# Chunk sums in two halves around the second edge layer, slot messages in two buffers, window additions ahead of the comparison

## The reference

```python
h = jnp.maximum(_layernorm(x), 0.0)
for l in range(5):                                    # on x = h
    h = _leaky(x @ W1[l] + b1[l]) @ W2[l] + b2[l]
    e = _leaky(edge_attr @ We1[l] + be1[l]) @ We2[l] + be2[l]
    msg = h[src] * e * dot_scale[l]
    agg = jax.ops.segment_sum(msg, dst, num_segments=n)
    out = x + agg * res_w[l]
    x = layernorm(out) * ln_g[l] + ln_b[l]
# the result is the input x plus the last x
```

## Time and profile before

| | us |
|---|---|
| median of 3 runs | 6610.09 |
| lowest and highest | 6605.63, 6611.65 |
| the profiled execution | 6615.82 |
| its span | 6614.0 |
| PE, DVE, ACT, POOL busy | 5622.6, 5148.4, 1133.9, 4527.2 |

### The profile page before, as it was taken

One profiled execution on the slowest core, in us unless ns is written; L12 is line 12 of the kernel. 1 busy time (PEld: TensorE's weight loads), 2 busy tenths in 40 slices (PEclk: granted clock), 3 DMA queues, 4 the chain that ended last, 5 costly groups with the idle time before them and its releaser, 6 DMA issues.

```text
span 6614.0 us, 169076 instructions
## 1 busy us (share of the span) xinstructions
PE 5622.6 (85%) x63332; PEld 3676.7 (56%) x63333; DVE 5148.4 (78%) x7991; ACT 1133.9 (17%) x1726; POOL 4527.2 (68%) x4793
## 2 busy tenths in 40 slices
PE   6776899988888788888878888888898887888887
PEld 2223444456666555666655666655566665556665
DVE  8997544688887688888768888867888875888886
ACT  0000211111122211112211112221111222111111
POOL 5777777666677377777727777746777773777775
PEclk9997555799999799999979999988999997999998
DMA  3112399755566355656635655644565563666664
GB/s 135 26 26 47 78 240 242 185 131 138 138 148 152 96 132 136 142 141 154 159 80 133 145 143 143 162 112 116 129 147 142 148 161 78 139 147 156 151 171 110
DMA packets 733545, 886.20 MB, mean 134 GB/s; under 512 B 325488, under 2 KB 502976, under 8 KB 731568
## 3 DMA queue, kind: packets, MB, share of 16 engines
q1 hardware_dynamic: 568480, 703.64, 40.8%
q0 software_dynamic: 152144, 154.93, 12.4%
q10 hardware_dynamic: 12096, 16.53, 0.8%
HBM read 749.51 MB, written 125.06 MB: 132 GB/s over the span
## 4 chain that ended last, share of the span: by engine, by line
PE 54%; DVE 21%; issue 15%; DVEq 4%; ACT 3%; DMA 1%; POOL 0%; ACTq 0%; SPq 0%; POOLq 0%
PE bank L980 14%; PE bank L976 8%; PE bank L1029 7%; PE bank L1053 5%; PE bank L922 4%; PE bank L879 3%; DVE arena L1662 3%; PE bank L1016 3%; PE bank L860 2%; PE bank L845 2%; DVEq L1782 2%; DVE arena L1750 2%; ACT arena L1241 2%; DVE arena L1670 2%; DVE arena L1408 2%
## 5 line engine op out<-in xcount | busy, mean ns | idle before, releaser
L793 POOL DMA_INDIRECT arena<-h_rows,src x3855 | 3674.3, 953 | 1693.5 <-issue 1250.7
L980 PEld LDWEIGHTS bank<-w2s,arena 128*128 128x128 f32 x8960 | 1175.7, 210 | 772.3 <-DVE arena L1750 437.2
L980 PE MATMUL bank<-w2s,arena 128*128 128x128 f32 x8960 | 1307.0, 303 | 208.2 <-DVE arena L1750 191.4
L780 POOL DMA_INDIRECT slots<-arena,slot_index x792 | 787.2, 994 | 267.2 <-issue 241.3
L976 PE MATMUL bank<-nodes_state,edge_w 64*128 64x512 f32 x980 | 598.4, 693 | 307.3 <-DVE nodes_state L1718 142.6
L1053 PEld LDWEIGHTS bank<-arena 112*64 112x64 f32 x20160 | 640.4, 138 | 267.0 <-issue 245.1
L1053 PE MATMUL bank<-arena 112*64 112x64 f32 x20160 | 725.8, 225 | 60.1 <-issue 54.2
L976 PE MATMUL bank<-x_packed,edge_w 64*128 64x512 f32 x1260 | 740.1, 669 | 16.4 <-ACT std L1190 15.6
L1241 ACT ACTIVATE arena<-bank,tenth 128x512 f32<-128x512 f32 x490 | 335.5, 685 | 2296.6 <-PE bank L976 2296.6
L1662 DVE SCALAR_TENSOR_TENSOR arena<-bank,edge_w,arena 128x512 f32<-128x512 f32 x490 | 366.7, 748 | 424.1 <-ACT arena L1241 421.4
L1670 DVE TENSOR_TENSOR x_packed<-bank,slot_rel 128x2880 f32<-128x2880 f32 (+8 forms) x315 | 588.9, 1870 | 15.8 <-issue 15.8
(11 more groups left out here) (198 smaller groups left out, 5615.6 us busy)
## 6 DMA issues: line engine op xcount, KB each, us to landing
arena<-slot_pick SPq DMA_DIRECT2D x630, 448.0 KB
arena<-h_rows SPq DMA_DIRECT2D x630, 224.0 KB
x_packed<-slot_attr SPq DMA_DIRECT2D x630, 128.0 KB
nodes_state<-attr_t SPq DMA_DIRECT2D x485, 128.0 KB
arena<-h_rows,src POOLq DMA_INDIRECT x3855
slot_pick<-arena SPq DMA_DIRECT2D x126, 448.0 KB
x_packed<-slots SPq DMA_DIRECT2D x127, 136.0 KB, 4.9
slots<-arena SPq DMA_DIRECT2D x9, 1904.0 KB, 22.1
```

The source lines that it names most:

```text
L780: pool.indirect_dma_start(slots, bass.IndirectOffsetOnAxis(ap=slot_index[:, t:t + 1], axis=0), records[:, v, j, :], None).then_inc(record_ ...
L793: pool.indirect_dma_start(to[0:n, at:at + D], None, table, bass.IndirectOffsetOnAxis(ap=index[0:n, t:t + 1], axis=0)).then_inc(landed(t), 16)
L980: mm = pe.matmul(to[:, j * P:(j + 1) * P], acts[:, j * TILE:(j + 1) * TILE], w2s[:, :], start=True, stop=True)
```

## The change

The slot message gets a second buffer (`slot_msg`), in a part of SBUF that is free in the layers, and its writer no longer waits for sums. `chunk_sums` takes a range of its four parts: the first half of a step's sums stays where all of them were, the second half goes into the next step, behind the hidden layers and ahead of the second edge layer. At a chunk's end both halves are in the chunk's last step, the second behind the gathers. On VectorE the window additions, with the reading of the window's start, move ahead of "middle" and of the one-hot of places; that one-hot now waits for the chunk sums of the step before the last, whose places it overwrites.

```diff
--- before.py
+++ after.py
@@ -168,7 +168,7 @@
 
         x_packed = sb("x_packed", [P, NHALF])
         late, at = {}, 0
-        for name, n in dict(place=TPG * WMAX, tenth=HALF, attr=2 * HALF, x=TN, spill_pick=WMAX, spill_msg=HALF).items():
+        for name, n in dict(place=TPG * WMAX, tenth=HALF, attr=2 * HALF, x=TN, spill_pick=WMAX, spill_msg=HALF, msg=HALF).items():
             late[name] = x_packed[:, at:at + n]
             at += n
         assert at <= NHALF
@@ -257,6 +257,7 @@
         hid_tenth = [area("hid_tenth"), late["tenth"]]
         slot_e = area("slot_e")
         msg = area("msg").rearrange("p (k c) -> p k c", k=2)
+        slot_msg = [msg[:, 1, :], late["msg"]]
 
 
         WIDE = 4 * BUCKETS
@@ -1018,21 +1019,21 @@
                             if j == TPH - 1:
                                 mm.then_inc(win_ready, 1)
 
-                def chunk_sums(i):
+                def chunk_sums(i, begin, end):
                     c = i // BG
                     w = widths[c]
-                    for j in range(TPH):
+                    for j in range(begin, end):
                         for side in range(2):
                             at, k = (2 * j + side) * D, 2 * j + side
                             for half in range(2):
                                 slots_of = slice(half * D, (half + 1) * D)
-                                mm = pe.matmul(sum_ps[half][side * D:(side + 1) * D, 0:w], msg[slots_of, 1, at:at + D],
+                                mm = pe.matmul(sum_ps[half][side * D:(side + 1) * D, 0:w], slot_msg[i % 2][slots_of, at:at + D],
                                                slot_places[i % 2][slots_of, k * w:(k + 1) * w],
                                                start=(i % BG == 0 and j == 0),
                                                stop=(ends_chunk(i) and j == TPH - 1 and side == 1))
                                 if j == TPH - 1:
                                     mm.then_inc(sum_ready, 1)
-                    if ends_chunk(i):
+                    if ends_chunk(i) and end == TPH:
                         pe.wait_ge(spill_picked, l * CHUNKS + c + 1)
                         pe.wait_ge(spill_msg_ready, l + 1)
                         own_wait(pe, "pe")
@@ -1071,6 +1072,8 @@
                     if k is not None:
                         pe.wait_ge(slot_attr_landed[k % 2], 16 * (l * (NB // 2) + k // 2 + 1))
                         hidden_of(1, k, NB, slot_attr_in[:, k % 2, :])
+                    if b_at(s - 1) is not None and not ends_chunk(s - 1):
+                        chunk_sums(s - 1, TPH // 2, TPH)
                     now, m = a_at(s), a_at(s + 1)
                     if now == SPILL_AT:
                         pe.wait_ge(spill_msg_ready, l + 1)
@@ -1092,11 +1095,13 @@
                     if b_at(s) is not None:
                         if k is None:
                             own_wait(pe, "pe")
-                        chunk_sums(s)
+                        chunk_sums(s, 0, TPH // 2)
                     part("middle")
                     if k is not None:
                         pe.wait_ge(slot_e_biased, l * NB + k + 1)
                         gathered(k)
+                    if b_at(s) is not None and ends_chunk(s):
+                        chunk_sums(s, TPH // 2, TPH)
 
                 k = l + 1
 
@@ -1752,9 +1757,7 @@
                     if i is not None:
                         dve.wait_ge(slot_e_biased, l * NB + i + 1)
                         dve.wait_ge(source_ready, 2 * (l * NB + i + 1))
-                        if i > 0:
-                            dve.wait_ge(sum_ready, 4 * (l * (NB + CHUNKS) + i + i // BG))
-                        dve.tensor_tensor(msg[:, 1, :], slot_e, slot_ps[:, :], ALU.mult).then_inc(slot_msg_ready, 1)
+                        dve.tensor_tensor(slot_msg[i % 2], slot_e, slot_ps[:, :], ALU.mult).then_inc(slot_msg_ready, 1)
                     m, i = a_at(s + 1), b_at(s + 1)
                     if m is not None and m != SPILL_AT:
                         at = real(m) * TPG
@@ -1768,20 +1771,22 @@
                     if m is not None:
                         dve.wait_ge(e_ready, l * GA + m + 1)
                         edge_biased(e_ps[:, :], e_ps[:, :]).then_inc(e_biased, 1)
+                    if k is not None and k != SPILL_AT:
+                        group = GB0 + real(k)
+                        window_start[:] = [dve.value_load(start_i[0:1, 2 * group + side:2 * group + side + 1],
+                                                          min_val=0, max_val=NPAD) for side in range(2)]
+                        window_added(s, k)
                     part("middle")
                     if i is not None:
                         w = widths[i // BG]
+                        if i > 1:
+                            dve.wait_ge(sum_ready, 4 * (l * (NB + CHUNKS) + i - 1 + (i - 1) // BG))
                         one_hot(slot_places[i % 2][:, 0:TPG * w].rearrange("p (t w) -> p t w", w=w), TPG, w,
                                 slot_rel[:, i * TPG:(i + 1) * TPG])
                         if ends_chunk(i):
                             c = i // BG
                             t = 2 * c * SPILL_CAP // TILE
                             one_hot(spill_pick[:, 0:w].unsqueeze(1), 1, w, spill_rel[:, t:t + 1]).then_inc(spill_picked, 1)
-                    if k is not None and k != SPILL_AT:
-                        group = GB0 + real(k)
-                        window_start[:] = [dve.value_load(start_i[0:1, 2 * group + side:2 * group + side + 1],
-                                                          min_val=0, max_val=NPAD) for side in range(2)]
-                        window_added(s, k)
                     if ends_chunk(s):
                         chunk_added(s)
```

## The result

| | us |
|---|---|
| before: median (lowest to highest) | 6611.65 (6605.63 to 6620.89) |
| after: median of 5 runs (lowest to highest) | 6644.18 (6640.62 to 6656.99) |
| ratio of after to before, 95% interval | 1.0052 (1.0037 to 1.0067) |
| the profiled execution, its span | 6640.62, 6638.7 |

The change makes the kernel 0.5% slower. The prediction said 55 us faster; the time is inside its range and on the wrong side.

A forecast was written before the change was run, and what follows sets the result against it. TensorE and VectorE hand work to each other, neither full; a step is as long as the later one. Seams 0, plain steps 0, tile starts +72, steps behind -114, chunk ends -13: -55, so 6555 us, range 6480 to 6670.

The forecast's parts named there:

- The seams: Additional breaks between TensorE's blocks, 585 in all: taken as 0; other end one exposed 210 ns weight load each, 123 us.
- The rival built on the dear end: Slower by seams: every additional seam exposes a weight load on TensorE, -55 + 123, giving 6678 us; chance 0.05.
- slower by uncovered loads: Rival: TensorE's edge block ends as VectorE reaches the bias, register loads lie open; +50, 6660 us; chance 0.15.
- The additions: VectorE's window additions moved ahead of the one-hot, freeing TensorE's next hidden layer earlier; whole forecast with seams at 0: -55 us.
- Plain steps: About 230 steps without node-tile part or chunk end, four kinds by windows: +22, +24, 0, -48 us, together about 0.
- Tile's first step: Where a node tile begins, 60 slots: three slot loads on VectorE lie open, 1.2 us more each, +72 us.
- The steps behind it: Two steps after a node tile's start: waits go, between 0.5 and 3.3 us a slot, middle 1.9, -114 us.
- Chunk ends: 45 chunk ends: 1.31 us of open loads goes, TensorE's later sums take over, 0.3 us left each, -13 us.
- The comparison's new wait: VectorE's one-hot comparison now waits for the sums of the step before last: 0.
- The additions' wait for the window sums: VectorE's additions wait for window sums 0.8 us behind the edge block, less than the loads take: 0 more.
- TensorE has room: Rival: TensorE has headroom, all slots give 3.3 us and plain steps lose all waits; -229, 6381 us; chance 0.12.
- The signs: Right: L1662 idle under 200 us, additions' "issue" 150 or more. Wrong: bias waiting over 300 us, or 0.1 us gaps.

The follow-up runs named there:

- f1: Kernel before with only VectorE's window additions and their register loads moved ahead of the one-hots, sums unsplit, one message buffer: 6540.9 us, ratio 0.9885.
- f3: Changed kernel with the next window's two registers loaded at the end of the step before: 6619.4 us, ratio 1.0010 to the kernel before.
- f4: As f3, and VectorE also reads the three slot registers at the end of a tile's first step: 6626.2 us, ratio 1.0016.
- i7: Changed kernel with the second half of the chunk sums behind the same step's gathers in every step, not between the layers: 6642.4 us, ratio 1.0047.
- i6: As f3, but the chunk sums in one piece at their old place, two message buffers kept: 6529.4 us, ratio 0.9872.

## Why the prediction was wrong, point by point

**The seams** are the step that failed: "The block of L1029 at 3812.92 takes 1.90 us and L1053 starts at 3814.75, with no gap. I take 0". The rows were read rightly and the conclusion doesn't follow. No gap is drawn because the next block starts 0.07 us before the drawn end; the price lies inside a block, in what a piece takes beyond its matmuls, and can be read by comparing pieces of different length or from the starts of single matmuls. The trace of before held no second length of the chunk sums, but it held the starts, and these give it: at width 360 the fours start 0.30 us apart, the first four keep the second for 0.35, and the last four keep the next block for 0.41, as in the kernels after. The other end that the prediction kept, 0.21 us x 585 = 123, was the nearer one: of the 103 us that splitting cost (6540.9 to 6644.2) the breaks are some 80 (the prediction's 585 left out the 40 at chunk ends), and the other 20 or so, the order at a chunk's end, were in the forecast's sum. Forecast and result differ by 88 us (-55 against +33, 6611.65 to 6644.18), and the breaks are nearly all of that. The rival built on the dear end is the one that came true by its mechanism, at +33 instead of +68 because a break costs less than 0.21 us and doesn't always show. It had been given 0.05. By the time alone "slower by uncovered loads" (6660) lies nearer to 6644, but the loads are not what costs, as f1, f3 and f4 show. The rule of the Trainium skill that was set aside ("TensorE: Matmul & The Clock Gate", Part 3, "The mechanism": a weight load overlaps matmuls in flight only where the row group differs) speaks for the dear end, which was the nearer one. The trace agrees with the rule only in part. At a piece's end the next block's first weight load starts with its matmuls (in i7 at 3492.452 and 3492.454, where the last load of the piece started at 3491.761). Within the piece, though, the loads start 0.30 us ahead of their own matmuls (width 360; 0.002 at a piece's first four), while matmuls on the same rows run. Whether it is the weight load or the block ahead running out that makes a piece's 0.16, no run here shows.

**The additions** were right in direction and nearly in size. The prediction said -55 with the breaks at nothing, the order at a chunk's end included. Measured alone the additions are worth -74 (6540.9 against 6615.1 on that chip), and with the 20 us or so of that order -54 (an estimate from the steps). That it came so near is in part luck: a tile's first step was put 44 us too dear and the steps behind it 51 us too favourable, and the two cancel. By its parts, with the table of the first section:
- Plain steps, predicted +22, +24, 0, -48: with the additions alone +9 (55 x 0.16), +19 (60 x 0.32), +7 and -31, together +5 where the prediction had 0. The two kinds whose wait the loads lengthen and the one that gains were all named rightly.
- Tile's first step, predicted +72: the idle time ahead of these 60 one-hots grew by 59 us (28.3 to 86.9) with the additions alone, but the steps only by 28 (55 x 0.50). The rest must have come out of other waits; which ones isn't shown. In the kernel after that idle time is 1.72 to 1.75 us in 9 of the third loop's 12, at one of them:

```profile
3738.09 2.56 DVE L1675 TENSOR_TENSOR x_packed<-bank,slot_rel 128x2304 f32<-128x2304 f32 x1 [1.73 <-issue]
```

- The steps behind it, predicted -114: -63 alone (260 steps, 8.30 to 8.06), -29 with the break. The slot that was worked out, priced at 3.3 us, gave more: the three steps around (between the starts of slot messages at 3808.71 and 3839.21) take 30.5 us before, 26.3 with the additions alone, 25.7 after. It was favourable, as the text said, and the middle of 0.5 and 3.3 was still too high: 63 / 55 = 1.1 us a slot.
- Chunk ends, predicted -13: -19 after. TensorE took over, as said. The row that answers to the earlier trace rows waits 0.42 us where it waited 1.31:

```profile
3537.69 2.31 DVE L1736 TENSOR_TENSOR nodes_state<-nodes_state,bank 64x360 f32 x4 [0.42 <-PE bank L1044]
```

  Without the sums behind the gathers the same steps gain 43 us (f1), so here the split took 24, of which the breaks are 6. The prediction's -13 has that delay in it. The step behind a chunk's end, not in the sum, adds 8 alone and 16 after.
- The comparison's new wait, predicted 0: in i6 the profile puts 30 us of idle time to it (13.2 and 17.2, L1030, ahead of the two groups of L1675). The one-hots wait no longer in total than in f3 (108 us in both), and i6 is no slower than f1 (6529.4 and 6540.9).
- The additions' wait for the window sums, predicted as less than the loads take: with the loads moved away they still wait 146.5 us in f3 and 133.6 in i6, 76.4 and 64.7 of it for L1017. So part of what the loads had covered was a wait that stays without them.

**The rivals.** "Slower by uncovered loads" had the loads' idle time right (1.0 us ahead of the additions; the row at 3480.36 of the kernel after says 0.86) and its worth wrong: 25 us with the break (f3), and no more than the intervals without (f1 to i6, 12 us). "TensorE has room" rested on weight loads at 63%; of 0.16 us more on TensorE in each step 0.12 to 0.13 came through in the steps that end no chunk, so it has little.

```profile
3480.36 0.60 DVE L1723 TENSOR_TENSOR nodes_state<-nodes_state,bank 64x80 f32 x2 [0.86 <-issue]
```

**The signs** it gave: L1662's idle time under 200 (218 came), more "issue" ahead of the additions and one-hots (came: 89 us for 63 and 94 for 28, though 150 were said for the additions), a bias over 300 us as the sign of slower (232 came, and it was slower), gaps of 0.1 us at the new seam (none came, and the seam was the cause). The last two were the wrong places to look; the chunk sums' own busy time, 1048 to 1194 us with the same matmuls, would have been the sign.

## What to carry to other kernels

The row of small matmuls here has a price by the piece, 0.16 us, beside that by the matmul, and a timeline without gaps says nothing of it: before a block is cut in two, compare a short and a long block of the same kind, T(32) against 2 x T(16). Where two engines hand work to each other in every step, most of what is added to one of them can come through though it looks idle 12% of the time: here 0.12 to 0.13 of 0.16 us. And when a sum of small prices hits the measured total, look at where the time was lost too: here a quarter of it lay in 40 steps of 630. Idle time ahead of an instruction is no gain to be collected: taking 155 us of it away brought 25 here, so ask first what the engine would wait for next.
